# The split keys' transfers to memory, issued by ScalarE instead of by SyncE

## The chip, the core and the metric

One NeuronCore of a Trainium2 chip runs the whole program as one launch. The metric is the device time of that launch in microseconds: the median of several runs. Engines are called PE (TensorE), DVE (VectorE), ACT (ScalarE), POOL (GpSimd) and SP (SyncE). DMA transfers are put into queues by an issuing engine and carried out by 16 DMA engines.

## The reference

Two layers on x of shape (8, 512, 128). Each normalises x, computes an attention branch s and a mixture-of-experts branch g, and returns x + s * silu(g). The change touches the second layer's attention, and there the projection of queries, keys and values:

```
qkv = hidden_states @ Wqkv.T + bqkv
qkv = qkv.reshape(b, s, 3, NH, HD).transpose(2, 0, 3, 1, 4)
q, k, v = (qkv[0], qkv[1], qkv[2])
...
q_rot = q_rot * cos + _rotate_half(q_rot) * sin
k_rot = k_rot * cos + _rotate_half(k_rot) * sin
...
logits = jnp.einsum('bhqd,bhkd->bhqk', q, k) * scale
probs = jax.nn.softmax(logits + causal_mask, axis=-1)
L = jnp.eye(s, dtype=probs.dtype) - jnp.tril(probs, -1)
A = jax.scipy.linalg.solve_triangular(L, rhs, lower=True)
```

There are 16 heads of 8 channels, 8 batches of 512 tokens.

## The kernel before

The program is a row of stages, each a block in which every engine has its own instruction stream, with semaphores between the streams, and a barrier of all engines at the end. The stage of this change is `project_qkv` (line 808). It takes the normalised activations, transposed, and writes three tensors to memory that the attention stage reads: `vT_dram`, `q_stack` and `k_stack`. The two stacks hold float32 queries and keys as three bf16 parts each (high, middle, low), six rows of parts for each channel, so that the logits can be computed with bf16 matmuls at float32 accuracy.

For each of the 8 batches:

- PE does five 128x512 matmuls (line 870): queries, their rotated twin, keys, theirs, values.
- DVE combines a projection with its twin (`rotate`, lines 893 to 900), once for queries (i = 0), once for keys (i = 1). The result is in `qk`.
- ACT copies `qk` to bf16, the high part (line 879). DVE subtracts it (line 916); what is left is in `rest`. ACT copies that to bf16, the middle part (line 886), and DVE subtracts again, which gives the low part (`lowest`, line 905). `lowest` of a batch comes in DVE's order behind `rotate` of the next one. Between its high and middle copies ACT moves the values out of PSUM with their bias (line 883).

DVE's order is written out by hand and is: `rotate` of batch b, `lowest` of batch b-1, the two subtractions of the high part of batch b. ACT's order is: high copies, values, middle copies. All parts of all batches stay in one buffer, `split`, so nothing there is written twice.

SP issues the transfers, in this order: eight pads of constant ones into `k_stack` (line 840, 16 partitions each, 256 KB), then values in pairs of batches (line 844, 512 KB), and behind the values of a pair the stacks of a group of batches that is complete by then. The groups are batches 0-1, 2-4 and 5-7:

```
GROUPS = ((0, 2), (2, 5), (5, B))
```

For a group SP waits for the low part of the group's last batch, then issues 12 transfers of queries (six part rows, two halves of 64 partitions) and then 12 of keys (line 852). Each has 64 partitions and a row of 512 bf16 values for each batch of the group: 128 KB in the first group, 192 KB in the others. SP ends with waits for everything to have landed (lines 854 to 857).

POOL scatters rows for the experts of this layer through its own queue meanwhile (`send`, line 496, 36 scatters here). The next stage begins behind the barrier, `solve_attention` (line 921); its first loads are masks, two experts' weights, then keys and queries from the stacks (lines 1046 and 1057).

Of the kernel before, what the change touches and what calls it, by code (L numbers as in the profile page):

```python
# [13 lines left out]
B, L, D = 8, 512, 128  # L14
# [6 lines left out]
HD = D // NH  # L21
# [7 lines left out]
K_PARTS = (0, 1, 2, 0, 1, 0)  # L29
Q_PARTS = (0, 0, 0, 1, 1, 2)  # L30
# [38 lines left out]
def tensors(nc, ctx):  # L69

    sems, stage = [], next(STAGES)

    def sb(name, shape, dt=F32):
        return ctx.enter_context(nc.sbuf_tensor(name, shape, dt))

    def sem(name):
        sems.append(nc.alloc_semaphore(f"{name}_{stage}"))
        return sems[-1]

    def clear():  # L80
        if sems:
            nc.clear_and_free_semaphores(sems)
            nc.all_engine_barrier()  # L83

    ctx.callback(clear)

    return sb, sem
# [616 lines left out]
class ExpertSteps:  # L704
# [86 lines left out]
    def send(self, pool, k):  # L791
        n = k % self.NO
        pool.wait_ge(self.x_in[k % self.NX], 16 * (k // self.NX + 1))
        if k >= self.NO:
            pool.wait_ge(self.o_out[n], 32 * (k // self.NO))
        self.nc.gpsimd.tensor_copy(self.to[n][:, :], self.xt[k % self.NX][:, :, D:D + 1].bitcast(U32).rearrange("p j a -> p (j a)")).then_inc(self.to_done, 1)
        pool.wait_ge(self.o_done, k + 1)
        pool.wait_ge(self.to_done, k + 1)
        for j in range(2):
            self.nc.gpsimd.indirect_dma_start(self.o_dram, bass.IndirectOffsetOnAxis(self.to[n][:, j:j + 1], 0),  # L800
                                              self.o[n][:, j, :], None).then_inc(self.o_out[n], 16)
# [6 lines left out]
def project_qkv(nc, xnT, wT, wsT, bias, rot, w_in, bank, k_stack, q_stack, vT_dram, send):  # L808

    with ExitStack() as ctx:
        sb, sem = tensors(nc, ctx)
        part = sb("rot_part", [P, 2, L])
        qk = sb("qk", [P, 2, 2, L])
        rest = sb("qk_rest", [P, 2, 2, L])
        split = sb("qk_split", [P, 2, B, 3, L], BF16)
        v = sb("v_chunk", [P, 2, 2, L])  # L820
        pad = sb("pad", [PAD, NSLOT * L], BF16)
        mm, rotated = sem("qkv_mm"), sem("rotated")
        hi_done, rest_done, mid_done, split_done = sem("hi_done"), sem("rest_done"), sem("mid_done"), sem("split_done")
        part_done, v_done, v_out = sem("part_done"), sem("v_done"), [sem(f"v_out{i}") for i in range(2)]
        stacked = sem("stacked")
        ones_set, pad_out = sem("ones_set"), sem("pad_out")
        block = ctx.enter_context(nc.Block())

        @block.gpsimd
        def _(pool):  # L830
            nc.gpsimd.memset(pad[:, :], 1.0).then_inc(ones_set, 1)
            send(pool)

        GROUPS = ((0, 2), (2, 5), (5, B))

        @block.sync
        def _(sp):
            sp.wait_ge(ones_set, 1)
            for b in range(B):
                sp.dma_start(k_stack[b, :, ROWS:].rearrange("h r s t -> r h (s t)"),  # L840
                             pad[:, :].rearrange("p (a q) -> p a q", a=1).broadcast_to([PAD, 2, NSLOT * L])).then_inc(pad_out, 16)
            for n in range(B // 2):
                sp.wait_ge(v_done, 2 * n + 2)
                sp.dma_start(vT_dram[:, 2 * n * L:(2 * n + 2) * L], v[:, n % 2, :, :].rearrange("p b t -> p (b t)")).then_inc(v_out[n % 2], 16)
                for b0, b1 in GROUPS:
                    if b1 not in (2 * n + 1, 2 * n + 2):
                        continue
                    for i, (stack, parts) in enumerate(((q_stack, Q_PARTS), (k_stack, K_PARTS))):
                        sp.wait_ge(split_done, 2 * (b1 - 1) + i + 1)
                        for term, p in enumerate(parts):  # L850
                            for hh in range(2):
                                sp.dma_start(stack[b0:b1, hh, term * HD:(term + 1) * HD].rearrange("b d s t -> (d s) b t"),
                                             split[64 * hh:64 * hh + 64, i, b0:b1, p, :]).then_inc(stacked, 16)
            for i in range(2):
                sp.wait_ge(v_out[i], 16 * (B // 4))
            sp.wait_ge(stacked, 16 * 4 * len(K_PARTS) * len(GROUPS))
            sp.wait_ge(pad_out, 16 * B)

        @block.tensor
        def _(pe):  # L860
            pe.wait_ge(w_in, 64)
            for b in range(B):
                rhs = xnT[:, b * L:(b + 1) * L]
                for n, i in enumerate((0, 3, 1, 4, 2)):
                    if b and n in (0, 2):
                        pe.wait_ge(rotated, 2 * b - 1 + n // 2)
                    if b and n == 4:
                        pe.wait_ge(v_done, b)
                    lhsT = wT[:, i * D:(i + 1) * D] if i < 3 else wsT[:, (i - 3) * D:(i - 2) * D]
                    nc.tensor.matmul(bank[i][:, :], lhsT, rhs, start=True, stop=True).then_inc(mm, 1)  # L870

        @block.scalar
        def _(act):
            act.wait_ge(w_in, 64)
            for b in range(B):
                n = b // 2
                for i in range(2):
                    act.wait_ge(rotated, 2 * b + i + 1)
                    nc.scalar.copy(split[:, i, b, 0, :], qk[:, i, b % 2, :]).then_inc(hi_done, 1)
                act.wait_ge(mm, 5 * b + 5)  # L880
                if b >= 4:
                    act.wait_ge(v_out[n % 2], 16 * (n // 2))
                nc.scalar.activation(v[:, n % 2, b % 2, :], bank[2][:, :], ACT.Identity, bias=bias[:, 2:3]).then_inc(v_done, 1)
                for i in range(2):
                    act.wait_ge(rest_done, 2 * b + i + 1)
                    nc.scalar.copy(split[:, i, b, 1, :], rest[:, i, b % 2, :]).then_inc(mid_done, 1)

        @block.vector
        def _(dve):
            def rotate(b, i):  # L890
                d = qk[:, i, b % 2, :]
                dve.wait_ge(mm, 5 * b + 2 * i + 2)
                nc.vector.scalar_tensor_tensor(out=d, in0=bank[i][:, :], scalar=bias[:, i:i + 1], in1=rot[:, 0, :],
                                               op0=ALU.add, op1=ALU.mult)
                if b or i:
                    dve.wait_ge(rotated, 2 * b + i)
                nc.vector.scalar_tensor_tensor(out=part[:, i, :], in0=bank[3 + i][:, :], scalar=bias[:, 3 + i:4 + i],
                                               in1=rot[:, 1, :], op0=ALU.add, op1=ALU.mult).then_inc(part_done, 1)
                dve.wait_ge(part_done, 2 * b + i + 1)
                nc.vector.tensor_tensor(d, d, part[:, i, :], ALU.add).then_inc(rotated, 1)  # L900

            def lowest(b):
                for i in range(2):
                    dve.wait_ge(mid_done, 2 * b + i + 1)
                    nc.vector.tensor_tensor(split[:, i, b, 2, :], rest[:, i, b % 2, :],
                                            split[:, i, b, 1, :], ALU.subtract).then_inc(split_done, 1)

            dve.wait_ge(w_in, 64)
            for b in range(B):
                rotate(b, 0)  # L910
                rotate(b, 1)
                if b:
                    lowest(b - 1)
                for i in range(2):
                    dve.wait_ge(hi_done, 2 * b + i + 1)
                    nc.vector.tensor_tensor(rest[:, i, b % 2, :], qk[:, i, b % 2, :], split[:, i, b, 0, :],
                                            ALU.subtract).then_inc(rest_done, 1)
            lowest(B - 1)
# [689 lines left out]
```

## Time and profile before

| | |
|---|---|
| median of 3 runs | 1444.02 us (1443.77 to 1447.59) |
| the profiled execution | 1442.47 us |
| its span (first to last instruction) | 1440.6 us |
| PE busy | 972.7 us (68%) |
| DVE busy | 866.7 us (60%) |
| ACT busy | 466.9 us (32%) |
| hardware queue (SP's issues), share of 16 DMA engines | 39.2%, 143.79 MB |
| software queue (POOL's scatters), share of 16 DMA engines | 4.0%, 19.02 MB |

The shares are averages over all stages. All times below are in us from the start of the span of this one profiled execution. `project_qkv` computes from about 398 to 455. A row of a timeline gives start, duration, engine, line, operation, what is written and read, how many instructions are merged, and in brackets how long the engine was idle before and what ended that. SPq is SP's queue of issues: its durations are those of issuing, not of the transfer. A row of a stretch gives its bounds and length, the busy time and instructions (x) of each engine, PE's granted clock as a share of full speed, the share of the DMA engines' time that packets took, and the rate at which bytes moved.

### The profile page before, as it was taken

The numbers are of one execution on the slowest core, as the hardware profiler recorded it, in microseconds if no ns is written. First come the engines' busy times: TensorE is split into PE (matmuls) and PEld (weight loads), VectorE is DVE, ScalarE is ACT, GpSimd is POOL, SyncE is SP. The second block draws the span as 40 slices with busy tenths as digits, with TensorE's granted clock in tenths as the row PEclk, the third lists the DMA queues.
The fourth block names the chain that finished last, engine by engine and source line by source line (L and its number), as shares of the span: only waits on it lengthen the run. The fifth ranks groups of instructions, "written<-read, shape, count | busy, mean of one in ns | idle before, by whom it ended". The sixth has DMA issues, their size and how long they took to land. (4 is left out here: it accounts for less than half of the span.)

```text
span 1440.6 us, 29654 instructions
## 1 busy us (share of the span) xinstructions
PE 972.7 (68%) x10741; PEld 760.5 (53%) x10762; DVE 866.7 (60%) x3503; ACT 466.9 (32%) x1066; POOL 344.1 (24%) x406
## 2 busy tenths in 40 slices
PE   5476699942473138677759777759967759967651
PEld 5265599942331025466636466536656647756541
DVE  5566362218786146666868766868857760056766
ACT  2233344425232003221135421135522218922124
POOL 0277255530074360022110022200002220012220
PEclk9798799985597588868779968779967869968776
DMA  9491699825088746511036420045521006521026
GB/s 218 93 249 51 174 252 239 232 73 141 24 129 262 212 123 165 133 35 28 13 96 159 111 64 27 13 111 145 141 61 38 28 23 193 147 72 34 17 70 175
DMA packets 256177, 164.71 MB, mean 114 GB/s; under 512 B 80960, under 2 KB 238912, under 8 KB 255776
## 3 DMA queue, kind: packets, MB, share of 16 engines
q1 hardware_dynamic: 246880, 143.79, 39.2%
q0 software_dynamic: 9152, 19.02, 4.0%
q8 instruction: 86, 1.41, 0.4%
q14 instruction: 59, 0.48, 0.1%
HBM read 99.12 MB, written 63.63 MB: 113 GB/s over the span
## 5 line engine op out<-in xcount | busy, mean ns | idle before, releaser
L1181 DVE TENSOR_REDUCE mx<-banks 128x1 f32<-128x384 f32 (+3 forms) x352 | 202.8, 635 | 70.9 <-PE banks L1113 59.1
L1336 DVE TENSOR_TENSOR prod<-A,Kst_Pn 128x8 f32<-128x8 f32 (+30 forms) x992 | 179.9, 222 | 8.9 <-POOL A L1290 8.5
L1342 DVE TENSOR_REDUCE A<-prod 128x4 f32<-128x8 f32 (+30 forms) x992 | 174.9, 217 | 0.0
L800 POOL DMA_INDIRECT o_dram<-step_o,step_to x80 | 81.1, 1013 | 287.3 <-ACT step_o L789 275.1
L1161 ACT ACTIVATE Eoff_RT_hidden<-banks 128x256 f32<-128x256 f32 (+2 forms) x192 | 114.9, 599 | 100.5 <-PE banks L1098 91.3
L1096 PE MATMUL banks<-Qexp,Kst_Pn 128*128 128x256 bf16 x640 | 114.8, 281 | 45.3 <-DMA Qmax<-q_stack 38.5
L1163 ACT ACTIVATE Ed<-banks 128x256 f32<-128x256 f32 x256 | 97.9, 382 | 123.0 <-PE banks L1098 123.0
L1109 PE MATMUL banks<-masks,identb 128*128 128x128 bf16 (+2 forms) x352 | 88.3, 251 | 65.7 <-DMA Qmax<-q_stack 54.1
L756 PE MATMUL banks<-step_xT,step_w 128*128 128x256 f32 x320 | 106.6, 491 | 22.5 <-issue 21.9
L1285 POOL TENSOR_TENSOR A<-A,Kst_Pn 128x256 f32<-128x256 f32 x16 | 14.1, 881 | 441.8 <-DVE Rb L1321 427.4
L1113 PE MATMUL banks<-Kst_Pn,Qmax 128*128 128x128 bf16 (+3 forms) x491 | 114.1, 302 | 0.0
L767 PE MATMUL banks<-step_w,step_h 128*128 128x128 f32 x640 | 90.6, 300 | 27.9 <-ACT step_h L782 27.9
L767 PEld LDWEIGHTS banks<-step_w,step_h 128*128 128x128 f32 x640 | 82.6, 209 | 48.5 <-ACT step_h L782 48.5
L1096 PEld LDWEIGHTS banks<-Qexp,Kst_Pn 128*128 128x128 bf16 x640 | 56.0, 100 | 83.0 <-DMA Qmax<-q_stack 40.9
L756 PEld LDWEIGHTS banks<-step_xT,step_w 128*128 128x128 f32 x320 | 74.8, 246 | 46.3 <-issue 34.0
L596 POOL DMA_INDIRECT o_dram<-e_o,e_to x78 | 76.6, 983 | 91.2 <-DVE e_o L617 79.0
L1233 PE MATMUL banks<-ident_c,Ed 32*128 32x32 f32 x512 | 74.5, 327 | 33.5 <-PEq L83 33.5
L1233 PEld LDWEIGHTS banks<-ident_c,Ed 32*128 32x128 f32 x512 | 73.1, 253 | 34.8 <-issue 34.3
L587 ACT ACTIVATE e_h<-banks,e_b 128x256 f32<-128x256 f32 x156 | 63.2, 471 | 80.1 <-PE banks L557 80.1
L1109 PEld LDWEIGHTS banks<-masks,identb 128*128 128x128 bf16 x352 | 34.9, 99 | 85.5 <-DMA Qmax<-q_stack 57.1
L557 PE MATMUL banks<-e_xT,e_w 128*128 128x256 f32 x312 | 76.2, 388 | 4.4 <-DMA e_b<-in_L_ffn_b_dram 3.8
L775 ACT COPY step_xT<-banks 128x256 f32<-128x256 f32 x40 | 15.0, 375 | 197.7 <-PE banks L745 197.6
(191 smaller groups left out, 1798.2 us busy)
## 6 DMA issues: line engine op xcount, KB each, us to landing
Kst_Pn<-k_stack SPq DMA_DIRECT2D x32, 512.0 KB, 4.4
rows_dram<-blank SPq DMA_DIRECT2D x12, 858.0 KB, 11.6
e_w<-in_L_w1T_dram SPq DMA_DIRECT2D x39, 256.0 KB, 3.1
e_w<-in_L_w2T_dram SPq DMA_DIRECT2D x39, 256.0 KB, 3.6
c_r<-o_dram SPq DMA_DIRECT2D x32, 256.0 KB, 5.1
sum_dram<-Eoff_RT_hidden SPq DMA_DIRECT2D x32, 256.0 KB, 4.0
Qmax<-q_stack SPq DMA_DIRECT2D x64, 96.0 KB
Qexp<-q_stack SPq DMA_DIRECT2D x64, 96.0 KB
```

Of the source, the lines that this page charges most:

```text
L756: last = self.nc.tensor.matmul(self.up_banks[i][:, (hc % 2) * TS:(hc % 2 + 1) * TS], self.w1[e % 2][:, hc * P:(hc + 1) * P], self.xT[:, :] ...
L767: last = self.nc.tensor.matmul(self.down_bank[:, j * D:(j + 1) * D], self.h[:, hc, j * P:(j + 1) * P], self.w2[e % 2][:, hc, :], start=(hc ...
L800: self.nc.gpsimd.indirect_dma_start(self.o_dram, bass.IndirectOffsetOnAxis(self.to[n][:, j:j + 1], 0), self.o[n][:, j, :], None).then_inc( ...
L1096: last = nc.tensor.matmul(out, Kst[b % 2][:, s, J * P:(J + 1) * P], Qexp[b % 2][:, 2 * s:2 * s + 2, :], start=True, stop=(J < I), skip_gro ...
L1109: nc.tensor.matmul(diagonal, identb[:, :], masks[:, 0:1, :].broadcast_to([P, per_bank, P]), start=True, stop=False, skip_group_check=True)
L1113: last = nc.tensor.matmul(out[:, j * keys_ahead:(j + 1) * keys_ahead], Qmax[b % 2][:, h, :], Kst[b % 2][:, h // 2, 0:keys_ahead], start=Fa ...
L1161: nc.scalar.activation(Eoff[:, n % 4, 0:I, :, :].rearrange("p j h q -> p (j h q)"), big[n % n_big][:, 0:I * 2 * P], ACT.Exp, scale=scale)
L1163: nc.scalar.activation(Ed[:, :, :].rearrange("p (g t) q -> p g t q", g=4)[:, 2 * (n % 2):2 * (n % 2) + 2, n // 2, :], big[n % n_big][:, I ...
L1181: nc.vector.tensor_reduce(out, logits, AX_X, ALU.max, negate=True).then_inc(max_done, 1)
L1233: last = nc.tensor.transpose(bank[g % 2][:, i * SUB:(i + 1) * SUB], Ed[ks, :, g * TURN + i], ident[ks, ks])
L1336: nc.vector.tensor_tensor(prod[:, ds, 0:r + 1], A[:, ds, k0:k0 + r + 1], Pn[:, c * SUB + r:c * SUB + r + 1, 0:r + 1].broadcast_to([P, HD / ...
L1342: nc.vector.tensor_reduce(A[:, ds, k0 + r], prod[:, ds, 0:r + 1], AX_X, ALU.add).then_inc(row_done, 1)
```

## The change

The key transfers leave SP's stream. ACT's stream gets a function `stack_keys`, called behind the middle copies of each batch and once at the end. It does something only where a group of batches is complete: it waits until DVE has split the group, and issues the group's 12 key transfers. They count on a semaphore of their own, `keys_stacked`, for which ACT waits at the end of the stage. SP keeps the pads, the values and the queries.

```
@@ project_qkv, sync
                 for b0, b1 in GROUPS:
                     if b1 not in (2 * n + 1, 2 * n + 2):
                         continue
-                    for i, (stack, parts) in enumerate(((q_stack, Q_PARTS), (k_stack, K_PARTS))):
-                        sp.wait_ge(split_done, 2 * (b1 - 1) + i + 1)
-                        for term, p in enumerate(parts):
-                            for hh in range(2):
-                                sp.dma_start(stack[b0:b1, hh, term * HD:(term + 1) * HD].rearrange("b d s t -> (d s) b t"),
-                                             split[64 * hh:64 * hh + 64, i, b0:b1, p, :]).then_inc(stacked, 16)
+                    sp.wait_ge(split_done, 2 * (b1 - 1) + 1)
+                    for term, p in enumerate(Q_PARTS):
+                        for hh in range(2):
+                            sp.dma_start(q_stack[b0:b1, hh, term * HD:(term + 1) * HD].rearrange("b d s t -> (d s) b t"),
+                                         split[64 * hh:64 * hh + 64, 0, b0:b1, p, :]).then_inc(stacked, 16)
             for i in range(2):
                 sp.wait_ge(v_out[i], 16 * (B // 4))
-            sp.wait_ge(stacked, 16 * 4 * len(K_PARTS) * len(GROUPS))
+            sp.wait_ge(stacked, 16 * 2 * len(Q_PARTS) * len(GROUPS))
             sp.wait_ge(pad_out, 16 * B)
@@ project_qkv, scalar
         def _(act):
+            def stack_keys(b):
+                for b0, b1 in GROUPS:
+                    if b1 == b:
+                        act.wait_ge(split_done, 2 * b1)
+                        for term, p in enumerate(K_PARTS):
+                            for hh in range(2):
+                                nc.scalar.dma_start(k_stack[b0:b1, hh, term * HD:(term + 1) * HD].rearrange("b d s t -> (d s) b t"),
+                                                    split[64 * hh:64 * hh + 64, 1, b0:b1, p, :]).then_inc(keys_stacked, 16)
+
             act.wait_ge(w_in, 64)
             for b in range(B):
...
                 for i in range(2):
                     act.wait_ge(rest_done, 2 * b + i + 1)
                     nc.scalar.copy(split[:, i, b, 1, :], rest[:, i, b % 2, :]).then_inc(mid_done, 1)
+                stack_keys(b)
+            stack_keys(B)
+            act.wait_ge(keys_stacked, 16 * 2 * len(K_PARTS) * len(GROUPS))
```

ACT's order around the end of the first group, from the high copies of batch 2 to the middle copies of batch 3, before (64x2x512 and the like are partitions and elements, x12 the number of instructions in a row):

```order
L879 CAST qk_split<-qk 128x512 x2
L883 ACTIVATE v_chunk<-banks,qkv_bias 128x512
L886 CAST qk_split<-qk_rest 128x512 x2
L879 CAST qk_split<-qk 128x512 x2
L883 ACTIVATE v_chunk<-banks,qkv_bias 128x512
L886 CAST qk_split<-qk_rest 128x512 x2
```

and with the change, where lines up to 879 and those behind it have moved by some numbers:

```order
L887 CAST qk_split<-qk 128x512 x2
L891 ACTIVATE v_chunk<-banks,qkv_bias 128x512
L894 CAST qk_split<-qk_rest 128x512 x2
L879 DMA k_stack<-qk_split 64x2x512 x12
L887 CAST qk_split<-qk 128x512 x2
L891 ACTIVATE v_chunk<-banks,qkv_bias 128x512
L894 CAST qk_split<-qk_rest 128x512 x2
```

The 12 key transfers of the first group now stand ahead of all copies of batch 3; those of the second group stand in the same way between batches 5 and 6, those of the third behind batch 7.

SP's queue from the pads to the end of the stage, before:

```order
L840 DMA k_stack<-pad 16x2x4096 x8
L844 DMA vT_dram<-v_chunk 128x1024
L852 DMA q_stack<-qk_split 64x2x512 x12
L852 DMA k_stack<-qk_split 64x2x512 x12
L844 DMA vT_dram<-v_chunk 128x1024 x2
L852 DMA q_stack<-qk_split 64x3x512 x12
L852 DMA k_stack<-qk_split 64x3x512 x12
L844 DMA vT_dram<-v_chunk 128x1024
L852 DMA q_stack<-qk_split 64x3x512 x12
L852 DMA k_stack<-qk_split 64x3x512 x12
```

and with the change:

```order
L840 DMA k_stack<-pad 16x2x4096 x8
L844 DMA vT_dram<-v_chunk 128x1024
L851 DMA q_stack<-qk_split 64x2x512 x12
L844 DMA vT_dram<-v_chunk 128x1024 x2
L851 DMA q_stack<-qk_split 64x3x512 x12
L844 DMA vT_dram<-v_chunk 128x1024
L851 DMA q_stack<-qk_split 64x3x512 x12
```

The three rows of keys are gone; the order of the others is the same.

## Rows read from the trace of the kernel before

**Rows 1.** Who waited, 449 to 500 us: total, times, longest, in us.

```profile
PE banks L1109 <- DMA Qmax<-q_stack: 48.8, 1, 48.8
...
DVE identb L970 <- PEq L83: 34.9, 1, 34.9
```

**Rows 2.** What SP's queue waited for, 484 to 492 us.

```profile
SPq L856 <- DMA k_stack<-qk_split: 2.4, 1, 2.4
```

**Rows 3.** Timeline of SP's queue, 395 to 500 us.

```profile
401.42 18.39 SPq L840 DMA_DIRECT2D k_stack<-pad  x8
...
422.90 12.43 SPq L852 DMA_DIRECT2D q_stack<-qk_split  x12
435.38 8.08 SPq L852 DMA_DIRECT2D k_stack<-qk_split  x12
...
457.17 8.93 SPq L852 DMA_DIRECT2D k_stack<-qk_split  x12
...
466.81 9.53 SPq L852 DMA_DIRECT2D q_stack<-qk_split  x12
476.38 8.81 SPq L852 DMA_DIRECT2D k_stack<-qk_split  x12
489.44 0.34 SPq L964 DMA_DIRECT2D Rb<-in_masks_dram  x1
```

**Rows 4.** SP's issues: stacks 422-424, 430-443, 466-490; pads (duration ns min/median/max).

```profile
L852 SPq DMA_DIRECT2D q_stack<-qk_split x1: 4345/4345/4345, 422.9 to 422.9; - x1
...
L852 SPq DMA_DIRECT2D k_stack<-qk_split x12: 607/612/753, 435.4 to 442.8; - x12
...
L852 SPq DMA_DIRECT2D k_stack<-qk_split x13: 621/708/774, 465.3 to 484.4; - x13
...
L840 SPq DMA_DIRECT2D k_stack<-pad x8: 330/2978/3269, 401.4 to 416.6; - x8
```

**Rows 5.** Stretches: busy us of PE, PEld, DVE, ACT, POOL; granted clock; DMA share; GB/s.

```profile
419.00:427.00 8.00, 6.33 (x15) 2.40 (x14) 7.93 (x13) 3.94 (x7) 6.17 (x7) 1.00 0.94 124
430.00:443.00 13.00, 9.65 (x22) 3.47 (x21) 12.86 (x21) 6.08 (x10) 10.26 (x10) 1.00 0.87 248
446.00:448.00 2.00, 0.35 (x1) 0.00 (x0) 2.00 (x4) 0.00 (x0) 1.70 (x2) 1.00 1.03 403
455.00:466.00 11.00, 0.00 (x0) 0.00 (x0) 0.00 (x0) 0.00 (x0) 0.00 (x0) 0.50 0.86 268
468.00:484.00 16.00, 0.00 (x0) 0.00 (x0) 0.00 (x0) 0.00 (x0) 0.00 (x0) 0.50 0.89 276
```

**Rows 6.** Timelines of ACT and then DVE: batches 2-3, 5-6, the last split.

```profile
420.15 1.22 ACT L886 CAST qk_split<-qk_rest 128x512 bf16<-128x512 f32 x2 [0.60 <-DVE qk_rest L916]
422.80 0.62 ACT L879 CAST qk_split<-qk 128x512 bf16<-128x512 f32 x1 [1.43 <-DVE qk L900]
...
429.30 0.62 ACT L879 CAST qk_split<-qk 128x512 bf16<-128x512 f32 x1 [1.43 <-DVE qk L900]
...
438.37 0.68 ACT L883 ACTIVATE v_chunk<-banks,qkv_bias 128x512 f32<-128x512 f32 x1
...
442.30 0.62 ACT L879 CAST qk_split<-qk 128x512 bf16<-128x512 f32 x1 [1.43 <-DVE qk L900]
...
445.44 1.28 DVE L916 TENSOR_TENSOR qk_rest<-qk,qk_split 128x512 f32<-128x512 f32 x2
...
453.31 1.29 DVE L905 TENSOR_TENSOR qk_split<-qk_rest,qk_split 128x512 bf16<-128x512 f32 x2
```

**Rows 7.** POOL's scatters alone (timeline, 495-512), with company (lines, 397-500); DVE's first rotation.

```profile
501.28 0.97 POOL L496 DMA_INDIRECT rows_dram<-Ed,slot  x1 [0.30 <-issue]
...
L496 POOL DMA_INDIRECT rows_dram<-Ed,slot x36 | 40.0, 1112 | 10.8 <-issue 10.8
...
L893 DVE SCALAR_TENSOR_TENSOR qk<-banks,qkv_bias,rot 128x512 f32<-128x512 f32 x16 | 11.9, 745 | 5.1 <-PE banks L870 5.1
```

**Rows 8.** PE's projection matmuls (line 870): duration ns min/median/max.

```profile
L870 PE MATMUL banks<-Ed,wqkvT x48: 592/592/1192, 397.9 to 449.5; 128*128 128x512 f32 x48
```

More of the change, by code:

```diff
@@ L824, in project_qkv @@
         part_done, v_done, v_out = sem("part_done"), sem("v_done"), [sem(f"v_out{i}") for i in range(2)]
-        stacked = sem("stacked")
+        stacked, keys_stacked = sem("stacked"), sem("keys_stacked")
         ones_set, pad_out = sem("ones_set"), sem("pad_out")
```

## The prediction

> **What bounds the kernel now.** The chain of waits only tells of the last stage, so I read who waited in the stretch that the change touches. When the query/key/value projection has finished computing, PE sits for 48.8 us until the first queries of the attention arrive, and DVE for 34.9 us at the barrier that ends the stage [rows 1]. What ends these waits is SP: it issues the last key transfer at about 485.2 us and then waits 2.4 us for it to land [rows 2], so the stage ends at 487.6 us, and the next stage's first instruction follows at 489.4 [rows 3]. Nothing after the barrier can start earlier, so what moves 487.6 moves the end of the program by the same amount. Engines are no bound here: the last DVE result of the stage is done at 454.6 us [rows 6], 33 us earlier.
>
> So the stage is a row of transfers, and the timeline of SP's queue shows them without a pause: eight pads, then for each group of batches V, 12 transfers of queries, 12 of keys [rows 3]. The durations of its issues say what paces them. SP's issues of keys take 607 ns at least, 612 in the middle of group 1 and 708 in group 3; a pad issue takes 330 ns when nothing is queued and 2978 in the middle, so **an issue waits when its queue is full**, and the issuing engine stands still for that time [rows 4]. The DMA engines are at a share of 0.86 to 0.89 while SP alone feeds them, with 268 to 276 GB/s [rows 5]. The work before the stage's end is therefore bytes over a rate, started early: SP's queue is never dry because compute runs ahead of it.
>
> **What moves.** The 36 key transfers (12 for each group) go from SP's queue into ScalarE's program: behind the copies of batch 2, of batch 5 and of batch 7. Bytes are the same: 24 x 128 KB = 3.15 MB in group 1, 24 x 192 KB = 4.72 MB in each of the others, 0.52 MB for each V transfer. SP loses 36 issues, about 26 us of its queue [rows 3]. One wait and one semaphore more at ScalarE's end cost nothing, since SP's last wait stands beside it. The new wait for the finished split holds nothing: DVE has made it one batch earlier, except behind batch 7.
>
> What it adds is that ScalarE stands still while it issues. Behind it are the next batch's copies; DVE waits for those, and on DVE hang the next splits. No row shows ScalarE issuing, so I bound the price. The nearest row is SP's for the same shape: 607 ns, and 8.08 us for 12 of them with the gaps in group 1, where the queue has room [rows 3], 0.67 each. The other end is POOL's issue of a scatter, 0.97 us with 0.30 idle before the next: 12 x 1.27 = 15.2 us [rows 7]. I take SP's, plus whatever wait for room the rate imposes. Nothing here lets it be under 607.
>
> **The rate with two queues** decides. At a share of 0.86 to 0.89 there is idle time; 268/0.86 and 276/0.89 both give about 310 GB/s for a share of one, my value. The ends: 268 (no gain), and 403, the best stretch beside it, with wider rows of V at a share of 1.03 [rows 5]. 403 is far off, since its rows in memory are 4 KB long where those of the split are 1 KB; 310 is nearer to the rows of the same transfers.
>
> A rule speaks against a gain. The profile's rows show the DMA engines nearly filled by one queue. The Trainium skill (DMA: Bandwidth & Descriptors, "Issuing engines are not separate DMA queues") says that DMAs from scalar, sync and gpsimd run on the same 16 DMA engines and interleave, and that several issuers only save sequencer time. By that rule the rate stays near 268 and the sum would be +13.5 us, the first rival below; by the rows there is a seventh of idle time to win, and it is +6.1. The trace of before does not show two hardware queues at once.
>
> **The sum**, in us of the profiled execution.
>
> Group 1. ScalarE's copies of batch 2 end at 421.4 [rows 6]; there it starts on keys. But the pads still fill the DMA engines (share 0.94 at only 124 GB/s from 419 to 427 [rows 5]), and SP's first query issue is held for 4345 ns until 427.2 [rows 4]. So from about 428 both halves, 3.15 MB, share 310 less POOL's 53 (248 GB/s [rows 5] less SP's 131 thousand bytes in each 0.67 us, which is 195): 257 GB/s, 12.3 us, landed at 440.3. An issuer is free 2.4 us before its last landing [rows 2]: 437.9. Before, the first copy of batch 3 started at 422.8 [rows 6]; now at 437.9, **15.1 late**. DVE uses 2.45 of that for work that it does not wait for (before, its two subtractions ended 4.4 after that first copy, at 446.7 against 442.3 in batch 6; now copy and subtractions, 0.62 + 1.3, are enough [rows 6]). V of batch 5 was finished at 439.05, that is 16.25 after the first copy of batch 3; now 437.9 + 16.25 - 2.45 = 451.7. Until then SP, which needs V of batch 5 first, has little to send.
>
> Group 2. From 451.7 on V and 24 transfers, 5.24 MB at 310 = 16.9 us, plus 1.2 to get going (in group 3 before: 20.8 us from first issue to landing [rows 2, 3] less 5.24 MB at 268 = 19.6). Landed at 469.8, ScalarE free at 467.4. The first copy of batch 6 follows at once; it began at 442.3 before.
>
> Group 3. From the first copy of batch 6 to the last split it was 12.3 us (454.6 less 442.3), less 2.45 again: 477.3. Then 4.72 MB, 15.2 + 1.2: landed at 493.7 instead of 487.6. **Sum: +6.1 us.** SP's shorter queue is paid back by three stretches in which compute and transfers take turns where they ran side by side.
>
> PE is not the next thing late: even a matmul at its slowest, 1192 ns [rows 8], makes 6.0 us for the five of a batch, under the 6.5 from batch to batch in ScalarE's copies [rows 6]. The granted clock falls to 0.50, the 1.2 GHz level, in the idle stretch from 455 on [rows 5]; it would fall in the new stalls too. Without that cover a restart would cost at most the 5.1 us that DVE waited for PE at the stage's own start [rows 7].
>
> The profiled execution took 1442.47 us (span 1440.6). With +6.1 it is 1448.6; the median of the runs stands 1.55 above that execution, so **1450.1**.
>
> **Rivals.**
> - *No gain of rate*: 268 GB/s with both queues. Group 1 at 268 - 53 = 215: ScalarE free at 440.3; group 2 from 454.1, free at 472.5; group 3 from 482.4, landed at 501.1: +13.5, 1457.5 in terms of the median. For it: the share of 0.86 to 0.89 has little left, and both issuers start with the same half of the partitions. Against: issues at the 607 floor in group 1, so the queue there had room.
> - *Keys pass beside the pads.* ScalarE's own queue gets its share at once and group 1 costs only 8.1 us of issuing: free at 429.5, group 2 from 443.3, free at 459.0, landed at 485.3: -2.3, 1441.7. For it: POOL's transfers keep flowing beside the pads (its 36 issues take 1112 ns on average, against 0.97 us without company [rows 7]). Against: those stretches have a share near one, and pads in front of SP's queue hold the engines.
> - *Faster: the rate rises to that of the V rows.* At 403, free at 434.6, group 2 from 448.4, free at 460.2, landed at 483.0: -4.6, 1439.4. It decides from about 355 GB/s on, where the sum crosses zero (in the inverse of the rate, between 310 and 403). For it: a second queue doubles what may be under way, and 403 was reached from 446 to 448 us. Against: rows of 1 KB did not come over 276 [rows 5].
> - *ScalarE issues at POOL's price*: 15.2 in each of groups 2 and 3: +8.6. It lies inside the range of the forecast.
>
> **How the numbers follow.** 0.3% (4.3 us) is about what a measurement of this kernel can tell from no change. The forecast has 0.50; its own range, for 335 down to 290 GB/s, is +2.5 to +9.3, and 0.15 of it lies within 0.3%. No gain of rate 0.17, slower. Keys beside the pads 0.17, within 0.3%. The higher rate 0.16, of which 0.03 within. So slower 0.35 + 0.17 = 0.52, same 0.15 + 0.17 + 0.03 = 0.35, faster 0.13. The range goes from the higher rate's 1439 to a little over the case without gain, 1459; about 2 in 10 lie outside, ScalarE's unseen issue price among them.
>
> **What would show it.** Right: in the timeline of ScalarE, three stretches with 12 key issues each and no copies, the first over 10 us long; DVE idle for that time before its subtraction of the high part; the DMA share low between the groups; the last issue between 488 and 492. The rate in groups 2 and 3 near 310 settles the second term. Wrong: ScalarE's issues at 0.67 us in all groups (then its queue takes more than SP's); over 355 GB/s in groups 2 and 3; or DVE without new waits. If the stage after the barrier changes its length, the assumption that everything behind shifts by the same amount has failed.

## The result and the profile after

The changed kernel takes **1456.78 us** (median of 6 runs, 1453.05 to 1460.79) where the kernel before takes 1443.89 (6 runs, 1442.19 to 1447.59). The ratio is 1.0087, 95% interval 1.0065 to 1.0109: slower by 12.9 us, in the direction forecast and inside the range, at about twice the forecast's +6.1.

The profiled execution is the longest of the six, 1460.79 us with a span of 1458.9, so its 18.3 us against the span before must be divided first. I take the stage from SP's first pad issue to SP's first issue of the next stage. Timeline of SP's queue, after (columns as in [rows 3]):

```profile
404.89 18.18 SPq L840 DMA_DIRECT2D k_stack<-pad  x8
423.11 3.15 SPq L844 DMA_DIRECT2D vT_dram<-v_chunk  x1
426.31 20.94 SPq L851 DMA_DIRECT2D q_stack<-qk_split  x12
447.29 11.27 SPq L844 DMA_DIRECT2D vT_dram<-v_chunk  x2
458.60 15.12 SPq L851 DMA_DIRECT2D q_stack<-qk_split  x12
483.33 0.33 SPq L844 DMA_DIRECT2D vT_dram<-v_chunk  x1
485.27 14.40 SPq L851 DMA_DIRECT2D q_stack<-qk_split  x12
506.27 0.34 SPq L975 DMA_DIRECT2D Rb<-in_masks_dram  x1
```

The stage lasted 489.44 - 401.42 = 88.0 us before [rows 3] and lasts 506.27 - 404.89 = **101.4** now. So 13.4 us lie in the stage; 3.5 lie ahead of it, in code that is the same, and 1.5 behind it. Executions differ by as much where the code is the same: in the thirteen profiled here the first matmul of the stage starts between 397.0 and 401.6 us, and what lies behind the stage lasts 948.5 to 953.0. The 13.4 is the change, and close to the 12.9 of the medians. SP had fewer issues and was done later: 12 query issues that took 9.5 us in group 3 before take 14.4 now, 12 that took 12.4 in group 1 take 20.9, and between groups the queue stands (the two V issues at 447.29 span 11.3 us).

Timeline of ACT, after, around the first and second group (ACTq is ACT's own issuing of transfers):

```profile
423.03 1.22 ACT L894 CAST qk_split<-qk_rest 128x512 bf16<-128x512 f32 x2 [0.60 <-DVE qk_rest L927]
423.64 20.75 ACTq L879 DMA_DIRECT2D k_stack<-qk_split  x12
444.43 1.14 ACT L887 CAST qk_split<-qk 128x512 bf16<-128x512 f32 x2 [20.18 <-issue]
...
459.41 16.57 ACTq L879 DMA_DIRECT2D k_stack<-qk_split  x12
476.03 1.14 ACT L887 CAST qk_split<-qk 128x512 bf16<-128x512 f32 x2 [16.00 <-issue]
...
485.88 16.29 ACTq L879 DMA_DIRECT2D k_stack<-qk_split  x12
```

For 20.75, 16.57 and 16.29 us ACT issues, and copies nothing. The copy of batch 3 that followed 1.4 us after the middle copies before [rows 6] now follows behind 12 issues. Who waited, 395 to 515 us, after (total, times, longest):

```profile
PE banks L1120 <- DMA Qmax<-q_stack: 35.1, 1, 35.1
...
PE banks L869 <- ACT v_chunk L891: 28.8, 2, 16.5
DVE qk_rest L927 <- ACT qk_split L887: 28.2, 2, 16.2
...
DVE identb L981 <- PEq L83: 20.5, 1, 20.5
```

Before, DVE waited for nothing from 415 us to its last split, then 34.9 us at the barrier [rows 1]. Now it waits 28.2 us for two high copies and 20.5 at the barrier. The wait has moved from the end, where it cost nothing, into the chain that the last transfers hang on. SP, the other issuer, stands too (what SP's queue waited for, after):

```profile
SPq L844 <- ACT v_chunk L891: 19.9, 2, 10.3
SPq L851 <- DVE qk_split L916: 4.8, 2, 2.6
SPq L855 <- DMA q_stack<-qk_split: 3.7, 1, 3.7
```

Stretches of the stage, after (columns as in [rows 5]):

```profile
452.00:458.00 6.00, 5.91 (x14) 2.28 (x13) 5.93 (x10) 2.84 (x5) 1.50 (x1) 0.97 0.07 23
461.00:474.00 13.00, 3.97 (x8) 1.36 (x8) 3.63 (x6) 0.00 (x0) 0.00 (x0) 0.82 1.00 277
478.00:485.00 7.00, 1.88 (x2) 0.31 (x2) 6.85 (x11) 3.70 (x7) 0.00 (x0) 0.50 0.13 51
488.00:500.00 12.00, 0.00 (x0) 0.00 (x0) 0.00 (x0) 0.00 (x0) 0.00 (x0) 0.50 1.01 278
```

Compute and transfers take turns: from 452 to 458 and from 478 to 485 DVE works and the DMA engines are at a share of 0.07 and 0.13; from 461 to 474 and from 488 to 500 it is the other way round. And in the stretches full of transfers, with two queues, the share has risen from 0.86 and 0.89 [rows 5] to 1.00, but the rate only from 268 and 276 to 277 and 278 GB/s. The DMA engines are busier at nearly the same rate of bytes.

### The profile page after: what moved, and what is told of

It is laid out like the page before. It is cut to its first block and busy times, and to the rows that moved or that the text cites. A ratio compares the mean times of both kernels' runs of the same rounds, so it can differ in the third digit from the quotient of the medians.

```text
span 1458.9 us, 29655 instructions
## 1 busy us (share of the span) xinstructions
PE 971.0 (67%) x10741; PEld 756.7 (52%) x10762; DVE 867.3 (59%) x3503; ACT 466.4 (32%) x1066; POOL 343.4 (24%) x406
## 5 line engine op out<-in xcount | busy, mean ns | idle before, releaser
L566 PE MATMUL banks<-e_w,e_h 128*128 128x128 f32 x624 | 75.9, 275 | 0.0
```

## The experiments

Three questions were open: is it ACT's standing still, or does a second queue cost something by itself; why did the rate not rise with the share; and why was the first stall 20.75 us where the others were 16.5. All times are medians; the ratio is against the kernel before on the same chip, with its 95% interval; the stage is measured as above, in the profiled execution (before: 88.0, the change: 101.4).

### ACT issues the last group alone

```
-                stack_keys(b)
             stack_keys(B)
-            act.wait_ge(keys_stacked, 16 * 2 * len(K_PARTS) * len(GROUPS))
+            act.wait_ge(keys_stacked, 16 * 2 * len(K_PARTS))
...
+                    if b1 < B:
+                        sp.wait_ge(split_done, 2 * b1)
+                        for term, p in enumerate(K_PARTS):
+                            for hh in range(2):
+                                sp.dma_start(k_stack[b0:b1, hh, term * HD:(term + 1) * HD].rearrange("b d s t -> (d s) b t"),
+                                             split[64 * hh:64 * hh + 64, 1, b0:b1, p, :]).then_inc(stacked, 16)
...
```

> ScalarE issues the keys of batches 5-7 alone, behind its last copy; SyncE keeps the keys of the first two groups. My theory (the loss is ScalarE standing still ahead of copies that DVE waits for, and two queues move no more bytes than one): no stall in ScalarE or DVE, stage end as in the kernel before, 0 to -1.5 us, about 1443. Rival A (issuing from two queues at once costs something itself, wherever it is done): the third group is as slow as in the change, +3 us or more. Rival B (two queues raise the rate to 310 GB/s where nothing waits for ScalarE): some 33 us of transfers from 454 us on shorten by about 4.4 us, 1439.5.

Measured: 1443.37 us, ratio 0.9995 (0.9979 to 1.0010); stage 87.2 us. DVE has no wait in the stage up to the barrier. From 458 to 474 us two queues are full, SP with keys of group 2 and ACT with keys of group 3 (this kernel's timeline of ACT, and the stretch):

```profile
455.93 16.11 ACTq L885 DMA_DIRECT2D k_stack<-qk_split  x12
...
458.00:474.00 16.00, 0.00 (x0) 0.00 (x0) 0.00 (x0) 0.00 (x0) 0.00 (x0) 0.50 0.99 273
```

It takes ACT the same 16 us as in the change, and costs nothing, since no copy stands behind it. The theory of the stall holds, rival A falls, and rival B falls with it: the rate in that stretch is 273 GB/s at a share of 0.99.

### All keys from ACT, behind the last copy

```
-                stack_keys(b)
-            stack_keys(B)
+            for b0, b1 in GROUPS:
+                stack_keys(b1)
```

> ScalarE issues all 36 key transfers, as in the change, but all behind its last copy of batch 7. My theory (stall, not queue): no copy stands behind an issue, DVE has no new wait and the last split is done at about 454.6 us; from there 8.65 MB are left at 276 GB/s, landed at about 487, so the time of the kernel before within 1.5 us (1442.5 to 1445.5). Rival A (the second queue itself costs): as the change, +9 us or more. Rival B (310 GB/s): -3 us or better.

Measured: 1445.51 us, ratio 1.0017 (1.0004 to 1.0031); stage 88.7 us. Against the change only the place of the issues in ACT's program differs (timeline of ACT, and a stretch):

```profile
453.70 33.17 ACTq L879 DMA_DIRECT2D k_stack<-qk_split  x36
...
456.00:484.00 28.00, 0.00 (x0) 0.00 (x0) 0.00 (x0) 0.00 (x0) 0.00 (x0) 0.50 0.92 257
```

36 issues of keys on ACT's queue, 33 us of standing still, and 0.2% where the change loses 0.9%. Together the two runs show that **where ACT issues is what costs**, not that it issues. What the remaining 0.2% is, no run shows: transfers that could have gone out before 454 us did not, and the rate from 456 to 484 is 257 GB/s where SP alone had 268 to 276 [rows 5].

### Opposite halves

```
-                            for hh in range(2):
+                            for hh in (1, 0):
...
```

> The change, but ScalarE's key transfers start with the upper half of the partitions while SyncE's query transfers start with the lower one. Theory P (the rate does not rise because both queues read the same half of the partitions at the same time): packets get shorter, the DMA rate in groups 2 and 3 rises from 275-278 GB/s to 300 or more, and the time falls by 4 us or more below the change, to 1452 or less. Theory M (the rate is set elsewhere, or the two queues drift against each other anyhow): rate within 3% of 277, time within 2 us of the change.

Measured: 1455.07 us, ratio 1.0087 (1.0064 to 1.0110); stage 99.8 us. The ratio is that of the change, and so is the rate (stretches of groups 2 and 3):

```profile
455.00:468.00 13.00, 3.97 (x8) 1.35 (x8) 3.61 (x6) 0.00 (x0) 0.00 (x0) 0.86 1.00 277
482.00:494.00 12.00, 0.00 (x0) 0.00 (x0) 0.00 (x0) 0.00 (x0) 0.00 (x0) 0.50 1.00 269
```

Taken alone this speaks for theory M, that the halves do not matter. It is a weak test: the order fixes only the first pair, and nothing in the program keeps the two queues in step behind it.

### All transfers from one half

```
-                                             split[64 * hh:64 * hh + 64, i, b0:b1, p, :]).then_inc(stacked, 16)
+                                             split[0:64, i, b0:b1, p, :]).then_inc(stacked, 16)
```

> The kernel before, but all stack transfers read the lower 64 partitions, so the heads of the upper half get the values of the lower half (this part of the computation is changed). Theory P (reading 64 partitions has a limit of its own, which only the alternation of halves hides): the rate in groups 2 and 3 falls from 268-276 GB/s towards 220 (16 partitions of pads gave about 112 together with other traffic), the stage gets 6 to 10 us longer. Theory M (writes to memory or the issue of each transfer set the rate): rate and time as in the kernel before, within 1.5 us.

Measured: 1458.83 us, ratio 1.0108 (1.0082 to 1.0135); stage 102.7 us, with SP alone issuing as in the kernel before. The rows of the upper heads then hold values of the lower ones; number, size and place of the transfers are the same. A stretch of group 3:

```profile
478.00:498.00 20.00, 0.00 (x0) 0.00 (x0) 0.00 (x0) 0.00 (x0) 0.00 (x0) 0.50 0.95 195
```

195 GB/s at a share of 0.95, where alternating halves gave 276 at 0.89 [rows 5]. Theory P: 64 neighbouring partitions have a limit of their own. The loss of 14.7 us is even above the 6 to 10 expected. The Trainium skill (SBUF — State Buffer, "Door 1: the DMA port swizzle") says that the DMA side has 16 ports and that partitions 0 to 63 reach only eight of them, 64 to 127 the other eight; for eight ports it gives a limit of about 218 GB/s. The run agrees in kind and shows 195.

### Even and odd heads on alternate partitions

The order of the channels is set on the host by a permutation of the weights. With the head's parity as the fastest index, the 64 partitions of a transfer are every second one of all 128:

```
-    order = np.arange(D).reshape(NSLOT, 2, HD).transpose(1, 2, 0)
-    swap = order[:, [1, 0, *range(2, HD)]].ravel()
+    order = np.arange(D).reshape(NSLOT, 2, HD).transpose(2, 0, 1)
+    swap = order[[1, 0, *range(2, HD)]].ravel()
...
-                                             split[64 * hh:64 * hh + 64, i, b0:b1, p, :]).then_inc(stacked, 16)
+                                             split[hh::2, i, b0:b1, p, :]).then_inc(stacked, 16)
```

and the rotation table in the same order. The places in memory stay the same; only the partitions that a transfer reads change. First in the kernel before:

> The kernel before, with the channels of even and odd heads on alternate partitions (weights and rotation table permuted), so that a transfer's 64 partitions are every second one of 128 instead of one half. Theory P (64 neighbouring partitions have a limit near 195 GB/s, and alternating halves hide it only in part): the rate of groups 2 and 3 with SyncE alone rises from 268-276 to about 300 GB/s, where the issue of 0.65 us for 192 KB limits it; 10 MB from 444 us on then take 3 to 4 us less, 1440. Theory M (memory's side or the engines themselves set 275): no change within 1.5 us.

Measured: 1438.34 us, ratio 0.9971 (0.9962 to 0.9981); stage 81.1 us. A stretch of groups 2 to 3:

```profile
462.00:478.00 16.00, 0.00 (x0) 0.00 (x0) 0.00 (x0) 0.00 (x0) 0.00 (x0) 0.50 0.93 316
```

316 GB/s with one queue, above what I had taken for two. V's 512 KB lie in this stretch; from 470 to 482 there are stack transfers alone, in this run and, second row, in the kernel before:

```profile
470.00:482.00 12.00, 0.00 (x0) 0.00 (x0) 0.00 (x0) 0.00 (x0) 0.00 (x0) 0.50 0.91 302
470.00:482.00 12.00, 0.00 (x0) 0.00 (x0) 0.00 (x0) 0.00 (x0) 0.00 (x0) 0.50 0.87 267
```

Then in the change:

> The change, with even and odd heads on alternate partitions as in the run before. Theory P: two queues then do reach 310 GB/s or more, and the term of my sum that was too small is the rate: groups 2 and 3 take 16 instead of 18 us each, the time falls 4 to 8 us below the change, to 1449-1453. It stays slower than the same layout with SyncE alone by 5 us or more, since ScalarE still stands still ahead of its copies. Theory M: as the change within 2 us, 1455 to 1457.

Measured: 1450.49 us, ratio 1.0047 (1.0033 to 1.0062); stage 92.4 us. The stalls of groups 2 and 3 fell to 13.15 and 12.27 us (timeline of ACT, and a stretch of group 3 with both queues full):

```profile
424.07 18.52 ACTq L879 DMA_DIRECT2D k_stack<-qk_split  x12
...
457.62 13.15 ACTq L879 DMA_DIRECT2D k_stack<-qk_split  x12
...
480.66 12.27 ACTq L879 DMA_DIRECT2D k_stack<-qk_split  x12
...
484.00:490.00 6.00, 0.00 (x0) 0.00 (x0) 0.00 (x0) 0.00 (x0) 0.00 (x0) 0.50 1.03 338
```

So here two queues move more than the 310 GB/s that the prediction assumed, and the change still loses: +4.4 us in the stage against the 88.0 of before. The prediction's sum with 340 GB/s and ACT free at 438.9, as it was here (442.6, less the 3.7 us by which this execution's copies start later), gives +4.2. Against the same layout with SP alone the stage is 11.3 us longer. And with ACT issuing where nothing waits for it:

> Even and odd heads on alternate partitions, and ScalarE issuing only the keys of the last group behind its last copy. Theory P: from 454 us on two queues move about 33 us worth of transfers at 310 to 340 GB/s, the stage ends 5 to 8 us earlier than in the kernel before, 1435.5 to 1438.5, faster than SyncE alone. Theory M: as the kernel before, 1443.

Measured: 1435.17 us, ratio 0.9953 (0.9940 to 0.9966); stage 79.7 us. That is 3.2 us under SP alone in this layout, though the two intervals still touch. Two full queues, this layout:

```profile
456.00:468.00 12.00, 0.00 (x0) 0.00 (x0) 0.00 (x0) 0.00 (x0) 0.00 (x0) 0.50 1.03 340
```

340 GB/s against 273 for the same two queues in the old layout. So theory P holds, and theory M, which the run with opposite halves had seemed to favour, falls: it was the choice of partitions.

### Pads from all partitions

```
-        pad = sb("pad", [PAD, NSLOT * L], BF16)
+        pad = sb("pad", [P, L], BF16)
...
-                sp.dma_start(k_stack[b, :, ROWS:].rearrange("h r s t -> r h (s t)"),
-                             pad[:, :].rearrange("p (a q) -> p a q", a=1).broadcast_to([PAD, 2, NSLOT * L])).then_inc(pad_out, 16)
+                sp.dma_start(k_stack[b, :, ROWS:].rearrange("h r s t -> (r s) h t"),
+                             pad[:, :].rearrange("p (a q) -> p a q", a=1).broadcast_to([P, 2, L])).then_inc(pad_out, 16)
```

> The change, with the pads read from 128 partitions instead of 16. If the pads in front of group 1 are what made ScalarE's first stall 20.75 us instead of about 16 as in groups 2 and 3: pads are out by about 412 us, the first stall falls to 12 to 15 us and the time by 5 to 8 us below the change, 1449 to 1452. If the first stall is only bytes over the rate with POOL's scatters beside it: the stall stays over 18 us and the time within 2.5 us of the change.

Measured, in the change: 1449.38 us, ratio 1.0049 (1.0036 to 1.0062); stage 96.7 us. SP's queue and ACT's first stall:

```profile
399.29 5.88 SPq L840 DMA_DIRECT2D k_stack<-pad  x8
413.86 0.33 SPq L844 DMA_DIRECT2D vT_dram<-v_chunk  x1
419.73 10.98 SPq L851 DMA_DIRECT2D q_stack<-qk_split  x12
```

```profile
421.54 12.45 ACTq L879 DMA_DIRECT2D k_stack<-qk_split  x12
434.03 1.14 ACT L887 CAST qk_split<-qk 128x512 bf16<-128x512 f32 x2 [11.88 <-issue]
```

Pads are issued in 5.9 us instead of 18.2, the first query goes out at 419.7, and the first stall is 12.45 instead of 20.75. So the pads in front of it made the first stall the longest: the rival in which keys pass beside the pads failed, and behind pads from 16 partitions the DMA engines were at a share of 0.94 with only 124 GB/s [rows 5].

POOL fills the smaller tile of ones sooner, so the first pad goes out 3.0 us earlier in the stage (timeline of POOL, the change and this run):

```profile
401.36 3.50 POOL L831 MEMSET pad<- 16x4096 bf16 x1 [23.22 <-POOLq L83]
398.74 0.53 POOL L831 MEMSET pad<- 128x512 bf16 x1 [22.89 <-POOLq L83]
```

A stage counted from the first pad therefore holds 3.0 us more in the runs with these pads; beside the others, 96.7 counts as 93.7. The kernel before with these pads:

> The kernel before with pads read from 128 partitions, nothing else changed. If pads hold the first group back: queries of group 1 are issued from about 420 us, SyncE has to wait for group 2 for some us at about 436, and the stage ends 5 to 7 us earlier, 1436 to 1438. If not: 1442.5.

Measured: 1439.47 us, ratio 0.9969 (0.9956 to 0.9983); stage 85.0 us, which counts as 82.0: a gain of 6.0, within the 5 to 7 expected, while the medians differ by 4.7. SP now waits 12.8 us for V of two pairs and 6.7 for splits: its queue stands for want of finished work.

### Both cures, with and without the stall

> The change with both causes of its slow transfers taken away (alternate partitions, pads from 128 partitions), while ScalarE still stands still ahead of batches 3 and 6. By my sum with the rate of 310 GB/s and a first group that starts at 421: ScalarE free at about 432 and 461, last landing at about 487, so 1441 to 1445, the time of the kernel before, and 12 us or more behind the version with the last group alone. If something else in the change costs: 1449 or more.

Measured: 1440.51 us, just under the 1441 to 1445 expected, ratio 0.9973 (0.9959 to 0.9987); stage 86.8 us. Stalls ahead of batches 3 and 6 remain (timeline of ACT):

```profile
424.01 10.37 ACTq L879 DMA_DIRECT2D k_stack<-qk_split  x12
...
449.40 12.71 ACTq L879 DMA_DIRECT2D k_stack<-qk_split  x12
```

The same transfers with ACT issuing the last group alone:

> Even and odd heads on alternate partitions, the keys of the last group alone from ScalarE, and pads read from 128 partitions: the version that the runs so far point to. If the three effects are separate: SyncE's first group starts at about 420 us instead of 427 and everything behind it moves up by 6 to 8 us against the version with slow pads (1435), to 1427 to 1430; DVE and ScalarE without new waits. If the pads only fill time in which nothing else is ready: no gain, 1435.

Measured: **1429.57 us**, ratio 0.9897 (0.9879 to 0.9916); stage 76.3 us. Timeline of its SP queue and, below, of ACT's:

```profile
400.08 5.91 SPq L840 DMA_DIRECT2D k_stack<-pad  x8
...
419.99 7.90 SPq L851 DMA_DIRECT2D q_stack<-qk_split  x12
427.93 7.78 SPq L857 DMA_DIRECT2D k_stack<-qk_split  x12
435.76 4.69 SPq L844 DMA_DIRECT2D vT_dram<-v_chunk  x2
...
459.45 13.09 SPq L851 DMA_DIRECT2D q_stack<-qk_split  x12
476.34 0.34 SPq L980 DMA_DIRECT2D Rb<-in_masks_dram  x1
```

```profile
455.67 12.59 ACTq L885 DMA_DIRECT2D k_stack<-qk_split  x12
```

This version beats both kernels: 1.03% faster than before, about 1.9% faster than the change (0.9897/1.0087 = 0.981). The 10.5 us between the last two stages (86.8 and 76.3) are the price of issuing ahead of copies, at full rate and without pads in the way; the medians are 10.9 apart, where 12 or more were expected. SP alone with both cures was not run, so what ACT's part is worth in this version is open.

## Why the prediction was right, and where it was too small

**Shown.** *Everything behind the barrier shifts by the stage's change.* The stage grew by 13.4 us, the median by 12.9. *ACT stands still and DVE with it.* DVE's waits were 16.2 and 12.0 us (28.2 in two); without an issue ahead of a copy they vanished, and with them the loss, although the second queue stayed in use (ratios 0.9995 and 1.0017). *The steps of the sum.* First copies of the stage, before and after:

```profile
404.02 0.62 ACT L879 CAST qk_split<-qk 128x512 bf16<-128x512 f32 x1 [18.33 <-DVE qk L900]
407.27 0.62 ACT L887 CAST qk_split<-qk 128x512 bf16<-128x512 f32 x1 [18.32 <-DVE qk L911]
```

They lie 3.3 us apart, and with that taken off ACT was free at 441.1 and 472.7 and the last split done at 482.6. From 441.1 on the prediction's steps with 277 GB/s give 472.6 and 482.5. So the chain is right, and with it the 1.2 us to get going, although that was misread: it counts V's bytes but starts at the first query issue (466.81), not at V's (466.14), from where it would be 1.9. *Compute and transfers take turns.* The DMA share falls to 0.07 and 0.13 between groups, as forecast. *PE's clock is no term.* It was granted 0.50, the 1.2 GHz level, from 478 to 485, when PE worked behind the second stall, but DVE's only new waits were for ACT.

**The step that failed is the rate with two queues**: 310 GB/s, from 268 and 276 divided by their shares. The share did rise to 1.00 and 1.01; the division assumed that a packet keeps its length. From the rows, 16 engines' share over the rate gives 52.6 ns of an engine for 1024 bytes before (0.86 at 268) and 59.5 now (1.01 at 278), so most of the gain in share went into longer packets. What takes its place is 277: with it the sum gives +11.7 us, and with the first group as measured, too, +13.1; 13.4 was measured in the stage. The first rival's +13.5 is nearer in part by luck: its 268 is under the measured rate, and its first group ended too early. That rival had 0.17 and should have had more, and the range held because it was drawn to take it in. That neighbouring partitions are the reason is shown by the runs on one half and on alternate partitions: 195, then 267, then 302 GB/s with one queue and stack transfers alone, and 273 against 340 with two. On alternate partitions the division does hold: 302 at a share of 0.91 makes 332 for a share of one, and two queues have 340 at 1.03, with 49.4 and 49.6 ns for 1024 bytes. Why the run with opposite halves gained nothing is not shown; that the queues drift apart within a group is only argued.

**The first group** was mis-sized as well. I freed ACT at 437.9; it was free at 444.4 - 3.3 = 441.1. Of those 3.2 us the sum at 277 GB/s (439.6) has 1.7; the other 1.5 are open. How far the pads reach into this stretch was the assumption under every sum; with them out of the way the stall is 12.45 instead of 20.75.

**The rule weighed there** came out in this layout. The Trainium skill (DMA: Bandwidth & Descriptors, "Issuing engines are not separate DMA queues") says that a second issuer saves sequencer time only. The trace agrees: the rate stayed at 277 to 278. On alternate partitions a second queue does bring something, 340 against 302, and one queue there leaves the share at 0.91. SP alone takes 7.9 to 8.0 us there to issue 12 transfers of group 3, no more than before where its queue had room (8.08 [rows 3]), which suggests that its issuing sets the pace and that this is what the second queue saves.

**The price of ACT's issue** was 588 ns at least, a little under the floor of 607 that I took from SP, and 1476 in the median, because its queue was full (issues of ACT in the change, duration ns min/median/max):

```profile
L879 ACTq DMA_DIRECT2D k_stack<-qk_split x36: 588/1476/4657, 423.6 to 500.8; - x36
```

Of the chance of 0.35 for no visible change, 0.17 rested on keys passing beside the pads, which the first stall of 20.75 us contradicts; the rest of it, and the 0.13 for faster, rested on the rate rising, and with partitions in halves it did not. The last issue, forecast between 488 and 492, was at about 502, or 499 with the later start taken off.

## What to carry to other kernels

An engine that issues transfers pays for the queue's fullness on top of the issue (here 1.48 us in the median, 0.59 at least): put issues on an engine only where nothing that others wait for stands behind them in its program, and compare "behind the last copy" with "between the copies" before judging a second queue. An idle share of the DMA engines is not a reserve until it is known what makes packets long; try which partitions a transfer reads before trying who issues it.

## What the runs showed of the hardware that was not expected

Transfers from the lower 64 partitions alone run at 195 GB/s, from alternating halves at 267 to 276, from every second of 128 partitions at 302 to 316 with one queue and 340 with two, with the same bytes and row length. Two queues on halves raise the DMA engines' share to 1.01 and the rate by under 4%. Pads of 2 MB from 16 partitions hold a queue for 18.4 us; from 128 partitions they are issued in 5.9.
